# The stacked queries of the second attention copied from SBUF to SBUF, without the round trip through DRAM

## What is computed

```
x = x + L0_xattn(layernorm(x), ctx)
x = x + L0_moe(layernorm(x))
q = layernorm(x) @ Wq.T + bq;  k = ctx @ Wk.T + bk;  v = ctx @ Wv.T + bv     # 16 heads of 8
attn = softmax(q k^T / sqrt(8));  x = x + (attn v) @ Wo.T + bo               # the change is here
x = x + L1_moe(layernorm(x))
```

## Time and profile before

| | |
|---|---|
| median of 3 executions | 363.34 us (363.33 to 364.29) |
| profiled execution | 362.01 us |
| its span, from first to last instruction | 360.0 us |
| mean granted TensorE clock | 0.935 |
| TensorE busy (matmuls) | 304.5 us, 85% |
| VectorE busy | 247.6 us, 69% |
| ScalarE busy | 191.9 us, 53% |
| GpSimd busy | 127.3 us, 35% |

### The profile page before, as it was taken

How to read it: one execution, slowest core, us unless ns; L and a number is a source line. 1 busy time by engine, 2 the same in 40 slices (tenths; PEclk the granted TensorE clock), 3 DMA queues, 4 the chain that set the end, 5 groups by cost and what they waited for, 6 DMA issues and landing times.

```text
span 360.0 us, 6232 instructions
## 1 busy us (share of the span) xinstructions
PE 304.5 (85%) x2260; PEld 208.2 (58%) x2260; DVE 247.6 (69%) x574; ACT 191.9 (53%) x351; POOL 127.3 (35%) x146
## 2 busy tenths in 40 slices
PE   2996839578888889984489999999898999999995
PEld 1675434367776777872125454545575777777773
DVE  3667896535566553458497788763779888998876
ACT  1364212133244324453226776786796888888881
POOL 5673455744313439063135301010103643254000
PEclk9998778969999999999557999999999999999998
DMA  7962392455564453501504100030000211000001
GB/s 217 280 240 88 77 187 29 31 64 120 135 137 84 98 135 16 172 5 46 117 20 114 34 5 2 3 121 1 0 2 0 83 36 58 1 2 0 0 3 58
DMA packets 12633, 25.37 MB, mean 70 GB/s; under 512 B 2051, under 2 KB 5403, under 8 KB 12347
## 3 DMA queue, kind: packets, MB, share of 16 engines
q1 hardware_dynamic: 11323, 22.22, 21.8%
q0 software_dynamic: 1024, 2.10, 6.8%
q10 hardware_dynamic: 256, 0.66, 0.6%
HBM read 20.94 MB, written 3.93 MB: 69 GB/s over the span
## 4 chain that ended last, share of the span: by engine, by line
PE 64%; DVE 16%; ACT 7%; DMA 5%; issue 4%; POOL 3%; SPq 0%; ACTq 0%; DVEq 0%; POOLq 0%
PE bank L757 56%; PE bank L966 3%; DVE score L1611 2%; PE bank L954 2%; DMA packc<-in_packc 2%; DMA big<-q_parts 1%; DMA xg<-normalised,slot_token 1%; DVE pbuf L1409 1%; PE bank L904 1%; POOL big L511 1%; POOL xg L501 1%; DVE xn L1278 1%; ACT gT L664 1%; POOL rstd L457 1%; PE bank L1109 1%
## 5 line engine op out<-in xcount | busy, mean ns | idle before, releaser
L757 PE MATMUL bank<-frbuf,splits 128*128 128x512 f32 x384 | 95.8, 399 | 1.3 <-DVE frbuf L1657 1.0
L757 PEld LDWEIGHTS bank<-frbuf,splits 128*128 128x128 f32 x384 | 69.7, 188 | 21.4 <-issue 5.3
L1657 DVE TENSOR_TENSOR frbuf<-pbuf,frbuf 128x512 fp32r<-128x512 f32 x64 | 52.5, 830 | 12.0 <-ACT pbuf L751 11.5
L501 POOL DMA_INDIRECT xg<-normalised,slot_token x32 | 34.2, 1070 | 50.5 <-DVE slot_token L1429 43.1
L1611 DVE TENSOR_REDUCE score<-bank 128x2 f32<-128x512 f32 x64 | 42.2, 688 | 14.4 <-PE bank L757 13.6
L747 ACT ACTIVATE frbuf<-bank,biases 128x512 fp32r<-128x512 f32 x64 | 44.2, 691 | 13.2 <-PE bank L757 9.8
L723 ACT ACTIVATE pbuf<-bank 128x512 f32<-128x512 f32 x64 | 37.1, 598 | 16.0 <-PE bank L757 15.6
L751 ACT ACTIVATE pbuf<-bank,biases 128x512 f32<-128x512 f32 x64 | 43.7, 683 | 0.0
L1435 DVE CAST splits<-bank 128x1024 fp32r<-128x1024 bf16 x16 | 19.6, 1224 | 31.6 <-PE bank L757 21.5
L757 PE MATMUL bank<-ks,big 128*128 128x256 bf16 x128 | 29.6, 323 | 6.3 <-DVE score L1611 3.7
L757 PE MATMUL bank<-splits,frbuf 128*128 128x512 f32 (+1 forms) x144 | 32.0, 373 | 0.8 <-ACT frbuf L668 0.8
(11 more groups left out here) (194 smaller groups left out, 492.5 us busy)
## 6 DMA issues: line engine op xcount, KB each, us to landing
big<-in_w SPq DMA_DIRECT2D x8, 704.0 KB
ew<-in_ew SPq DMA_DIRECT2D x16, 256.0 KB, 3.4
big<-in_w SPq DMA_DIRECT2D x8, 352.0 KB
ks<-k_parts SPq DMA_DIRECT2D x4, 512.0 KB, 8.9
k_parts<-parts SPq DMA_DIRECT2D x2, 768.0 KB, 4.5
big<-q_parts SPq DMA_DIRECT2D x8, 192.0 KB
x<-in_x SPq DMA_DIRECT2D x1, 512.0 KB, 5.3
k_parts<-parts SPq DMA_DIRECT2D x1, 512.0 KB, 2.8
```

Of the source, the lines that this page charges most:

```text
L501: pool.indirect_dma_start(out=xg[:, g % 2, j, :], out_offset=None, in_=xn_dram, in_offset=bass.IndirectOffsetOnAxis(ap=slot_token[:, g % 3 ...
L757: return pe.matmul(out_, lhsT, rhs, start=start, stop=stop, skip_group_check=True)
L1657: v.tensor_tensor(out=actl[:, n % NA, :], in0=act[:, n % 4, :], in1=acth[:, n % NA, :].bitcast(F32), op=ALU.subtract).then_inc(f_lo, 1)
```

## The change

The DRAM buffer `qscratch` and the semaphore `qd_out` go. Each combination of a batch is copied by a DMA of its own from the 128 partitions of `parts` to 8 partitions of `qs`, 64 KB each, with rows of 512 B; eight for a batch in place of five. In batch 0 SP issues the five of the high and low part, and ScalarE the three of the middle part, right behind its rounding of that part. In batches 1 to 3 SP issues all eight. Of the three DMAs of the first maxima, ScalarE issues two, right behind its copy to `nmT`. `max_scores` waits for 8 DMAs in place of 3.

```diff
-        qscratch = nc.dram_tensor("q_parts", [NB, 3, P, TB], BF16, kind="Internal").ap()
+        def queries_of_part(queue, b, j):
+            for i in range(NCOMB):
+                if PARTS_Q[i] == j:
+                    queue.dma_start(qs[i * HD:(i + 1) * HD, b, :, :],
+                                    parts[:, j, batch(b)]).then_inc(qs_in[b], 16)
+        def maxima_of_part(queue, k, part):
+            b, hs8 = k // 2, slice(k % 2 * 8, k % 2 * 8 + 8)
+            queue.dma_start(qs[KROWS + part:KROWS + part + 1, b, hs8, :],
+                            nmT[k % 2][part * 8:(part + 1) * 8, batch(b)]).then_inc(nm_in[k], 16)
...
             def queries_stacked(b):
                 sp.wait_ge(q1_hi, b + 1)
-                sp.wait_ge(q1_mid, b + 1)
-                sp.dma_start(qscratch[b, 0:2].rearrange("j p t -> p j t"),
-                             parts[:, 0:2, batch(b)]).then_inc(qd_out[b], 16)
+                queries_of_part(sp, b, 0)
+                if b >= 1:
+                    sp.wait_ge(q1_mid, b + 1)
+                    queries_of_part(sp, b, 1)
                 sp.wait_ge(q1_lo, b + 1)
-                sp.dma_start(qscratch[b, 2], parts[:, 2, batch(b)]).then_inc(qd_out[b], 16)
-                sp.wait_ge(qd_out[b], 32)
-                rows = qscratch[b].rearrange("j (d h) t -> (j d) h t", d=HD)
-                for i in range(0, NCOMB, 3):
-                    n = min(3, NCOMB - i)
-                    sp.dma_start(qs[i * HD:(i + n) * HD, b, :, :], rows[0:n * HD]
-                                 ).then_inc(qs_in[b], 16)
+                queries_of_part(sp, b, 2)
             def maxima_stacked(k):
                 sp.wait_ge(a_nmT, k + 1)
-                for part in range(3):
-                    sp.dma_start(...)
+                for part in range(3 if k else 1):
+                    maxima_of_part(sp, k, part)
...
                 a.copy(parts[:, 1, batch(b)], query_rest(b)).then_inc(q1_mid, 1)
+                if b == 0:
+                    a.wait_ge(q1_mid, 1)
+                    queries_of_part(a, b, 1)
...
                            ).then_inc(a_nmT, 1)
+                    if k == 0:
+                        a.wait_ge(a_nmT, 1)
+                        for part in (1, 2):
+                            maxima_of_part(a, k, part)
...
-                    pe.wait_ge(qs_in[b], 48)
+                    pe.wait_ge(qs_in[b], 16 * NCOMB)
```

More of the change, by code:

```diff
@@ L271, in build @@
             sem("q1_ps"), sem("q1_f"), sem("q1_hi"), sem("q1_res"), sem("q1_mid"), sem("q1_lo"))
-        qd_out, qs_in, nm_in = sems("qd_out", NB), sems("qs_in", NB), sems("nm_in", 2 * NB)
+        qs_in, nm_in = sems("qs_in", NB), sems("nm_in", 2 * NB)
         a_zero, a_S, a_max, a_nmp, a_nmTp, a_nmT, a_ST, a_exp = (
@@ L381, in queries_stacked @@
                 sp.wait_ge(q1_hi, b + 1)
-                sp.wait_ge(q1_mid, b + 1)
-                sp.dma_start(qscratch[b, 0:2].rearrange("j p t -> p j t"),
-                             parts[:, 0:2, batch(b)]).then_inc(qd_out[b], 16)
+                queries_of_part(sp, b, 0)
+                if b >= 1:
+                    sp.wait_ge(q1_mid, b + 1)
+                    queries_of_part(sp, b, 1)
                 sp.wait_ge(q1_lo, b + 1)
-                sp.dma_start(qscratch[b, 2], parts[:, 2, batch(b)]).then_inc(qd_out[b], 16)
-                sp.wait_ge(qd_out[b], 32)
-                rows = qscratch[b].rearrange("j (d h) t -> (j d) h t", d=HD)
-                for i in range(0, NCOMB, 3):
-                    n = min(3, NCOMB - i)
-                    sp.dma_start(qs[i * HD:(i + n) * HD, b, :, :], rows[0:n * HD]
-                                 ).then_inc(qs_in[b], 16)
+                queries_of_part(sp, b, 2)
             def maxima_stacked(k):
-                b, hs8 = k // 2, slice(k % 2 * 8, k % 2 * 8 + 8)
                 sp.wait_ge(a_nmT, k + 1)
-                for part in range(3):
-                    sp.dma_start(qs[KROWS + part:KROWS + part + 1, b, hs8, :],
-                                 nmT[k % 2][part * 8:(part + 1) * 8, batch(b)]
-                                 ).then_inc(nm_in[k], 16)
+                for part in range(3 if k else 1):
+                    maxima_of_part(sp, k, part)
             queries_stacked(0)
```

## The result

The changed kernel takes 370.31 us in the median of 4 executions (369.36 to 370.74), the kernel before 363.81 beside it. The ratio is 1.0172 (95% interval 1.0141 to 1.0203): slower, by some 6.5 us. The forecast was 361.8 us; the way that rival A described is the one that the trace shows.

What follows compares the result with a forecast made beforehand. TensorE, busy 85% of the span, was taken as the bound, with slot 0 held back by DMAs. Slot 0's -1.5 us and zero for the other terms took 363.34 to 361.8 us, range 360.5 to 365.4.

Steps and rivals of the forecast that it cites:

- rival A: Narrow query copies take 1.2 us each, one after another per queue, delaying maxima 2: +2.8 to +4.5 us; chance 0.23.
- What bounds the kernel: The slots run at TensorE's pace; slot 0 waits for the DMAs, and its 2.22 us of idle time can be won.
- Part 1: Batch 0's round trip: at 0.7 to 0.9 us per copy, the queries land at 171.5 to 173.
- Part 2: ScalarE's three issues of 0.67 us delay TensorE's last query product by 0.7; slot 0 starts at 173.3, 1.5 won.
- Part 3: First maxima: ScalarE's two issues of 0.67 us ahead of its table load are hidden by 2.1 us; no stall.
- Part 4: Batches 1 to 3 on SP: maxima 2 wait 0.8 us, margin 0.7 at exp_scores(16), so nothing is lost.
- Part 5: TensorE's clock around the first slots: effect taken as zero, with some 0.3 us lost or up to 0.6 won kept open.
- Sum: Whole kernel: -1.5 us at slot 0, zero for first maxima, batches 1 to 3 and clock; 363.34 becomes 361.8.

Runs made afterwards that it cites:

- stepped kernel: The changed kernel with each combination's 8 rows on every 4th partition, all copies and maxima issued by SP, none by ScalarE: 357.91 us, 1.0010 of the kernel before.

## Why the prediction was wrong

**What bounds the kernel**: right. Slot 0 waits for a DMA before and after, and from `exp_scores(16)` to the end the distance is 156.5 to 157.0 in every kernel but the one with all copies on SP (158.5): what the slots lose at their start is lost at the end.

**Part 1 failed**, in its price of a copy. I took 0.7 to 0.9 us, "nearer to the issue's pace, since successive DMAs write different partitions and can overlap". They hardly do: 60 GB/s, 1.09 us each, while an issue on SP takes 0.61 (0.64 taken). The sum all in a row gave 177.6 for the landing; measured is 178.23, or 177.5 without the 0.71 by which everything upstream was late. The upper bound was the result, but that the two agree to 0.1 is luck: with 1.09 the same sum gives 166.8 + 8.7 + 1.2 = 176.7, and the other 0.8 came from batch 1, as far as can be told. I set it aside although the only narrow transfers in the trace, the reads of 24 and 16 partitions, had taken the same 1.2. The split did not shorten it either: two queues together moved 61 GB/s, and ScalarE's three copies share that with batch 1's eight on SP. The term was -1.5 and measured +2.6 to +2.8.

The rule that was cited against this part held. By the Trainium skill, "SBUF — State Buffer", Door 1: The DMA port swizzle, the prediction had estimated 54 GB/s and 1.2 us for such a copy. The measured rate, 60 GB/s, is 11% above that estimate and is what counts. Rows on every 4th partition remove the cost (10.37 to 6.74), as reaching more ports by that rule should. The rule of the Trainium skill, "DMA: Bandwidth & Descriptors", Why a DMA increments its semaphore by 16 and not by 1, does not tell the two apart: both write 8 partitions from 128.

**Part 2**: the mechanism was right and the size was too small. Three issues took 2.74, not 2.0, because the first alone took 1.38. ScalarE's copy of batch 2's transpose then started at 170.56, and TensorE's product of batch 2 waited 2.48 for it. The last product ended at 174.69, 1.4 later than before without the 0.71 upstream; the forecast was 0.7. It decided nothing here, since the DMAs were later still. With the rows on every 4th partition it shows: slot 0 stands 7.64 behind the rest where ScalarE issues, and 7.11 where it does not.

**Part 3**: right. The two issues of the first maxima lie ahead of the table load, and `exp_scores(0)` stands 14.38 behind slot 0 as before.

**Part 4 failed** too, and twice. First in the place. The margin was worked out for maxima 2 behind batch 3, and the wait came one step sooner, at `exp_scores(8)`, with maxima 1 behind batch 2's eight copies. By rival A's own 1.2 us batch 2 moves until 195.3 and a landing 1.2 later is 196.5, where rival A, with 0.8 won, would have had `exp_scores(8)` at 195.8. So a stall of 0.7 stood in the text's numbers, and I followed only batch 3 from them.

Its size was 2.84, since the landing took longer as well. 189.42 + 0.61 + 8 x 1.09 is 198.8, plus 1.2 for a landing 200.0, and maxima 1 landed at 202.32. The packets themselves fit the sum: in the trace batch 2's last ends at 198.80 and those of maxima 1 by 199.05. It is the semaphore steps that are late, counted as before without the one at each issue: those of batch 2 until 200.79 and those of maxima 1 from 200.61 to 202.32, more than 3 us behind the packets at the last. In the stepped kernel with all on SP the last step of maxima 2 comes 0.45 behind its last packet (198.61 and 199.06). So behind narrow copies the 1.2 us from issue to landing do not hold. Why the steps come late is open.

Second, the sum was short even with the price that it assumed. With spread rows and the issues split as in the changed kernel, maxima 2 were ready at 193.44 and SP issued them at 195.48: they waited 2.0 for SP, where the sum had 0.8, and the margin of 0.7 became a stall of 1.61. It took back more than the 1.26 won at slot 0. So even with copies as cheap as forecast the 1.5 us do not come: that version measured 1.0005.

**Part 5**: "zero" was wrong, but by consequence. Rival A had named this price: the clock falls in the gap, "up to 1.7". It came to 2.63 and 1.33. Here TensorE idled for 2.84 us, the granted clock went to 0.50 (1.2 GHz) in the gap and came back at 208.4 after 6 us of dense work, and the distance to `exp_scores(16)` grew by 2.63. In the later session the same gap cost 1.33, with the low clock gone by 200.9:

```profile
197.40:200.90 3.50, 3.46 (x21) 1.49 (x22) 1.38 (x2) 2.03 (x4) 0.00 (x0) 0.56 0.65 64
200.90:204.00 3.10, 2.97 (x32) 1.48 (x32) 2.34 (x4) 2.03 (x4) 0.00 (x0) 1.00 0.39 37
```

Together with the distance to `exp_scores(8)`, idle times of 2.84 and 2.77 cost 4.9 and 3.8, 1.4 to 1.7 times themselves. The stepped kernel's 1.28 us at `exp_scores(16)` made that distance 1.45 longer, and its granted clock stayed at 1.00.

**Sum.** Forecast -1.5; rival A +2.8 to +4.5; measured +6.1 to +6.5. Rival A fell short because it counted batch 0 as won by 0.8, though its price of 1.2 in one row gives 177.6: three copies on another queue were taken as moved for free. It had the kind and the sign of the loss right, the seat only in part.

## What to carry to other kernels

Price an SBUF to SBUF copy by which partitions its narrower side touches, not by bytes, by DMA count or by their number alone: 64 KB onto 8 neighbouring partitions took 1.09 us here, on one queue or two, and eight such copies took 10.37 us where eight to every 4th partition took 6.74. Where a layout is free, as a contraction's row order is, spread it before a hop is removed. Then look at what is issued behind the copies on the same queue, and move the copies into a stretch in which the queue is idle: that order was worth 1.4 us at `exp_scores(16)`, the shorter path 1.9 at slot 0, and only the two together moved the total. Last, count on a small DMA behind such copies to land late: in the changed kernel its packets were done more than 3 us before its semaphore had its full count.

## What the runs showed beyond that

- The first DMA that ScalarE issued in the stretch took 1.38 us on its sequencer, the next two 0.64 and 0.67. SP's issues of the query copies took 0.61 in the median.
- Copies from 8 partitions to 128 are slow as well: 8.62 for eight, against 6.47 from 128 to 128.
- Reads from DRAM in two DMAs of 32 partitions took 4.46, in three of 24, 24 and 16 5.70, in one of 64 4.50. That 0.74 of it shows in the kernel, ahead of slot 0, and none of it in the total, is left open.
- A copy alone took 3.33 us, three times what it adds in a row of eight: (10.37 - 3.33) / 7 is 1.0.
